# Dealing out anew the side work of the attention heads in a fused attention and mixture-of-experts block

## The reference

```python
q, k, v = x @ Wq.T, x @ Wk.T, x @ Wv.T          # x is layer-normed; q 512 wide, k and v 128 wide
scores = einsum('bsqhd,bthd->bqhst', qh, kh) * scale   # 8 key heads of 16, 4 query groups each
a_dot  = einsum('bqhst,bthd->bsqhd', softmax(scores), vh)
sigma_q = elu(q.reshape(b, s, 4, 128))
a_mem  = sigma_q @ memory / (sigma_q @ memory_norm)
x = x + a_dot * (1 - w) + a_mem * w             # w = sigmoid(memory_weight)
# then: layernorm, router (sigmoid, top 4 of 16 experts), experts of 192, shared expert, sum
```

## Time and profile before

| | us |
|---|---|
| median of 3 executions | 1956.91 (1956.83 to 1957.64) |
| the profiled execution | 1947.51 |
| its span, first to last instruction | 1945.6 |
| PE busy | 1872.0 (96%) |
| DVE busy | 1031.1 (53%) |
| ACT busy | 978.7 (50%) |
| POOL busy | 921.2 (47%) |

### The profile page before, as it was taken

How to read it: one execution, slowest core, us unless ns; L and a number is a source line. 1 busy time by engine, 2 the same in 40 slices (tenths; PEclk the granted TensorE clock), 3 DMA queues, 4 the chain that set the end, 5 groups by cost and what they waited for, 6 DMA issues and landing times. The chain is left out here.

```text
span 1945.6 us, 34872 instructions
## 1 busy us (share of the span) xinstructions
PE 1872.0 (96%) x9240; PEld 965.8 (50%) x9241; DVE 1031.1 (53%) x1995; ACT 978.7 (50%) x1901; POOL 921.2 (47%) x1127
## 2 busy tenths in 40 slices
PE   6899999999999999999999899999999999999996
PEld 5444445444544454445333455555555555555553
DVE  5667777878787878787888252222221222222213
ACT  3366776677667766776766532223332233322330
POOL 3533566666666766675633650333333333333342
PEclk9799999999999999999999999999999999999998
DMA  6422334434443444333532897877777777777779
GB/s 193 108 70 64 83 94 132 128 107 116 132 134 103 116 131 135 104 103 120 150 120 82 290 342 237 183 142 141 141 144 142 142 141 141 143 143 141 142 164 262
DMA packets 159128, 277.71 MB, mean 143 GB/s; under 512 B 28704, under 2 KB 64800, under 8 KB 156256
## 3 DMA queue, kind: packets, MB, share of 16 engines
q1 hardware_dynamic: 108688, 147.61, 26.7%
q0 software_dynamic: 40880, 106.96, 26.6%
q10 hardware_dynamic: 9440, 21.68, 3.2%
HBM read 145.65 MB, written 135.74 MB: 145 GB/s over the span
## 5 line engine op out<-in xcount | busy, mean ns | idle before, releaser
L993 DVE TENSOR_REDUCE mx<-ps_max 128x2 f32<-128x1024 f32 x512 | 618.1, 1219 | 174.7 <-PE ps_max L1203 160.6
L732 ACT ACTIVATE prob<-ps_exp 128x512 f32<-128x512 f32 x992 | 566.9, 598 | 149.2 <-PE ps_exp L1217 131.6
L1948 PE MATMUL ps_gu<-wts_sb,xT 128*128 x1152 | 402.7, 493 | 1.2 <-issue 1.0
L1217 PE MATMUL ps_exp<-qs,ks 98*128 98x512 bf16 x992 | 380.0, 383 | 18.9 <-ACT prob L732 16.7
L1647 POOL DMA_INDIRECT out<-yt,idx x72 | 111.7, 1551 | 467.6 <-ACT yt L1716 453.2
L1203 PE MATMUL ps_max<-ks,qs 96*128 96x512 bf16 x1024 | 310.2, 385 | 7.5 <-DVE mx L993 4.0
L1828 DVE COPY hT<-ps_h 128x384 f32<-128x384 f32 x88 | 49.1, 557 | 463.2 <-PE ps_h L1957 463.2
L1948 PEld LDWEIGHTS ps_gu<-wts_sb,xT 128*128 128x128 f32 x1152 | 207.3, 190 | 170.9 <-issue 56.4
L1245 PE MATMUL ps_pv<-prob,vs 128*32 128x512 f32 x2048 | 251.8, 605 | 0.2 <-ACT prob L740 0.2
L1706 ACT ACTIVATE gs<-ps_gu 128x192 f32<-128x192 f32 x176 | 58.2, 330 | 376.4 <-PE ps_gu L1948 376.4
L1217 PEld LDWEIGHTS ps_exp<-qs,ks 98*128 98x128 bf16 x992 | 96.8, 98 | 195.7 <-ACT prob L732 88.5
(11 more groups left out here) (197 smaller groups left out, 2177.2 us busy)
## 6 DMA issues: line engine op xcount, KB each, us to landing
xt<-rows_by_expert SPq DMA_DIRECT2D x144, 264.5 KB, 2.7
dnr_sb<-in_dnr SPq DMA_DIRECT2D x144, 128.0 KB, 2.6
qk_parts<-parts POOLq DMA_DIRECT2D x112, 120.0 KB, 3.6
qs<-qk_parts SPq DMA_DIRECT2D x64, 192.0 KB, 3.1
wts_sb<-in_wts ACTq DMA_DIRECT2D x12, 1024.0 KB, 8.3
x_sb<-in_x SPq DMA_DIRECT2D x16, 512.0 KB, 4.5
qs<-qk_parts SPq DMA_DIRECT2D x64, 128.0 KB, 3.1
x_plus_memory<-am SPq DMA_DIRECT2D x16, 512.0 KB, 5.2
```

The source lines that it names most:

```text
L732: act.activation(prob[:, s, q], ps_exp[:, q % 2], ACT.Exp, scale=SCALE).then_inc(s_exp, 1)
L993: dve.tensor_reduce(mx[:, k % 2, 4 * s + 2 * p:4 * s + 2 * p + 2], ps_max[:, p], AX_X, ALU.max).then_inc(s_maxd, 1)
L1217: pe.matmul(ps_exp[:, q % 2], ks[0:ROWS + MROWS, kk, s * P:(s + 1) * P], qs[0:ROWS + MROWS, kk, q], start=True, stop=True).then_inc(s_sc, 1)
L1948: mm = pe.matmul(ps_gu[:, i, 0:2 * I], xT[:, i, d], w, start=(d == 0), stop=(d == DC - 1))
```

## The change

No arithmetic changes but for padding: the maxima's transposes become 128 wide, with zeros, where they were 32 wide. What changes is where work stands.

- **Transposed maxima.** `mb` is 128 wide (a memset more at the start), `max_T` writes into `ps_pv` and not `ps_misc`, and waits for ACT's copy of `ps_pv` (`s_oT`); the next `pv` at p = 4 waits for ACT's copy of the maxima (`s_mT`).
- **`o_T` and `o_out`** go from p = 3 to p = 2 in ordinary heads, `o_T` right behind `max_T`.
- **Rows' transposes.** `a_T` goes from places -12 and -11 (20 and 21) to -12 and -8 (20 and 24), `c_T` stays at 4 and 8; all stand ahead of the place's `pv` on PE (`ahead_of_pv`), where they stood behind it, and ACT copies them right behind the place's exponentials (`behind_exps`).
- **Values.** One piece of eight products at place -7 becomes three: two products each at -11 and -10 (first half of the rows) and four at -7.
- **Keys.** Two products each at -1 and 1 become one each at -3, -2, -1 and 1.
- **Logits.** Eight products at 9 become four at 9 and four at 11 (`logits_at`), with an exponential of 16 columns each on ACT.
- **Memory read.** Three rounds of 3, 3 and 2 products at 23, 28 and 29 become four rounds of 2 at 17, 19, 23 and 27; DVE has four copies for three. The first two rounds need only the first half of sigma.
- **ACT.** The second step of the elu (`below`) goes from 8.5 and 16.5 to right behind its first (7.5 and 15.5), ahead of `oT_out`.
- **DVE.** `weights` (four small linked instructions) goes from place 19 to 21.

```diff
-MEM = 3
+MEM = 4
-    mb = sb("mb", [P, 2, 2, 16], BF16)
+    mb = sb("mb", [P, 2, P], BF16)
-    USUAL = LAST | {"rank": 16}
+    USUAL = LAST | {"rank": 16, "weights": 21}
...
-    MEM_ROUNDS = [[(0, 0), (0, 1), (0, 2)], [(0, 3), (1, 0), (1, 1)], [(1, 2), (1, 3)]]
+    MEM_AT = (17, 19, 23, 27)
+    MEM_ROUNDS = [[(0, 2), (0, 3)], [(1, 2), (1, 3)], [(0, 0), (0, 1)], [(1, 0), (1, 1)]]
...
-                pe.wait_ge(s_sig, 2 * a + 2)
+                pe.wait_ge(s_sig, 2 * a + (1 if n < 2 else 2))
...
+                    pe.wait_ge(s_mT, min(g, NG))
...
             def max_T(g, k):
-                free_misc()
+                if g >= 3:
+                    pe.wait_ge(s_oT, g - 2)
                 pe.wait_ge(s_mb, g)
-                pe.transpose(misc_b[0:32, 0:P], mb[:, (k + 1) % 2].rearrange("p a n -> p (a n)"), identb[:]).then_inc(s_mTp, 1)
-                set_free(s_mT, g)
+                pe.transpose(pv_b[:, 0:P], mb[:, (k + 1) % 2], identb[:]).then_inc(s_mTp, 1)
...
+                        if p in (0, 4):
+                            at(ahead_of_pv(8 * k + p))
...
-                        if p == 2 and runs(g, 1, NG + 1):
-                            max_T(g, k)
-                        if p == 3 and runs(g, 3, NG + 3):
-                            o_T(g)
+                        if p == (3 if alone(g) else 2):
+                            if runs(g, 1, NG + 1):
+                                max_T(g, k)
+                            if runs(g, 3, NG + 3):
+                                o_T(g)
```

More of the change, by code:

```diff
@@ L144, in attention @@
     ps_pv = lent_ps("ps_pv", [P, SEQ])
-    misc_b = ps_misc[:, :].bitcast(BF16)
+    pv_b = ps_pv[:, :].bitcast(BF16)
     BANK_OF_T = [[ps_misc[:, :], ps_max[:, 0, 0]], [ps_max[:, 0, 1], ps_max[:, 1, 0]]]
@@ L711, in xn2T_out, with exp_logits @@
                                ACT.Copy).then_inc(s_xn2T, 1)
[L713 to L716, removed]
+            def exp_logits(t):
+                act.wait_ge(s_lg, 2 * c + (t + 1 if c < NU - 3 else 2))
+                act.activation(rt[:, 0, t], ps_misc[:, t * E:(t + 1) * E], ACT.Exp, scale=-1.0).then_inc(s_el, 1)
             at = places_of(c)
-            return {at["T"][0]: [lambda: xn2T_out(0)], at["T"][1]: [lambda: xn2T_out(1)], at["logits"]: [exp_logits]}
+            first, second = (behind_exps(p) if c < NU - 3 else p for p in at["T"])
+            return logits_at(c, exp_logits) | {first: [lambda: xn2T_out(0)], second: [lambda: xn2T_out(1)]}
         def body(b):
@@ L769, in body @@
                         at(8 * k + p)
-                        if p == 2 and runs(g, 1, NG + 1):
+                        if p == (3 if alone(g) else 2) and runs(g, 1, NG + 1):
                             mT_out(g, k)
@@ L1017, in body @@
                             maxima(g, k, s, half_)
-                        if p == 3 and runs(g, 3, NG + 3):
+                        if p == (3 if alone(g) else 2) and runs(g, 3, NG + 3):
                             o_out(g, k)
@@ L1069, in front @@
                     split(a, chunk)
-            for p in (23, 28, 29):
+            for p in MEM_AT:
                 for task in of_a(0)[p]:
@@ L1127, in a_q, with a_k @@
                     set_free(s_qf, 3 * a + (3, 2)[j])
[L1129 to L1131 removed]
+            def a_k(i):
+                if i == 0:
                     free_misc()
[L1133 to L1134 removed]
                     pe.wait_ge(s_xnT, 2 * a + 2)
[L1136 to L1138 removed]
+                mm = pe.matmul(ps_misc[:, 0:UT], w_sb[:, i, D:D + P], xnT[:, i], start=(i == 0), stop=(i == DC - 1))
+                if i == DC - 1:
                     mm.then_inc(s_proj, 1)
@@ L1188, in of_c @@
             at = places_of(c)
-            return {at["T"][0]: [lambda: c_T(0)], at["T"][1]: [lambda: c_T(1)], at["logits"]: [c_logits],
+            first, second = (ahead_of_pv(p) if c < NU - 3 else p for p in at["T"])
+            return logits_at(c, c_logits) | {first: [lambda: c_T(0)], second: [lambda: c_T(1)],
                     between_halves(at["rank"]) if c < NU - 3 else at["rank"]: [c_rank]}
```

122 lines of the change are left out of this document (63 added, 59 removed).

## The result

| | before | changed |
|---|---|---|
| median, us | 1957.28 (4 executions) | 2015.47 (2014.44 to 2020.14, 4 executions) |
| ratio | | 1.0298, 95% interval 1.0278 to 1.0318 |
| profiled execution / its span | 1947.51 / 1945.6 | 2014.67 / 2012.8 |
| PE, DVE, ACT, POOL busy | 1872.0, 1031.1, 978.7, 921.2 | 1881.3, 1043.0, 1005.1, 923.2 |

The forecast was 2008 in a range of 1970 to 2020. PE is busy for only 9 us more, and the span is 67 us longer: the time went into waits.

The account below looks back on a forecast made before the run. PE bounds the heads, busy 63.73 of 64.75 us; an ordinary block grows 4.5 to 69.2. Blocks 3 to 12 add 45, block 13 4, 14 and 15 3.5, 0 to 2 -1: +51 on 1956.9 gives 2008, range 1970 to 2020.

Parts of the forecast that it names:

- places 0 to 4: Block start: rows of c ahead of `pv` wait 2.7 us for POOL's norm; place 5 comes 2.3 later.
- 5 to 11, with the wait at 11: Copies, halved logits, maxima and a wait of 0.6 at place 11 make this stretch 0.4 us later.
- 17 to 20: Places 1.8, 1.7, 1.9 and 3.7 through waits for the bank and DVE; block 1.6 us later at place 21.
- 21 to 24: Weights and maxima delay DVE's memory copy; PE waits 1.5 at place 24; block 3.1 behind at 25, from 1.6.
- 25 to 31: Fewer values products, no memory at 28 and 29, and single keys, less a wait at 27: 1.3 us back.
- not stretched: Rival: chain at the block's start not stretched, wait at place 4 only 1.4, block 3.2 longer, 1995 us; chance 0.18.
- faster: Rival: PE finds the bank free at place 3, about 2.5 a block gained in 11 blocks, 1926 us; chance 0.08.
- DVE's queue is shorter: Rival: waits at 20 and 24 (1.9) fall to 0.5, block about 1.7 longer, 1977 us; chance 0.14.
- Four heads give back 0.6: Transposed maxima without 32-column products cost PE 0.11 for 0.26 a head, 0.6 us less a block.
- the order undone by the last units: Worse rival: the last units' other tables cost at most 10 us more, 2018 us; chance 0.08.
- The start stays: The kernel's start, like the experts, was taken to keep its time.
- About 35 us is the most that any dealing could give back: Upper limit from PE's waits of 2.7 us a block, in 10 full blocks and half a dozen with less.

Follow-up runs that it names:

- e1: Changed kernel with the first of unit c's two row transposes (place 4) back behind `pv`, ACT's copy too: 1971.8 us, ratio 1.014.
- e2: Changed kernel with POOL's addition of x at place 26, ahead of three scatters, not at 31: 1976.4 us, ratio 1.017.
- e7: Changed kernel with the edits of e1, e2 and e3 together: 1949.6 us, ratio to before 0.9975.
- e3: Changed kernel with DVE's weights at place 20 rather than 21: 1989.7 us, ratio 1.023.
- e5: Changed kernel with memory read in three rounds at 23, 28 and 29, not four at 17, 19, 23 and 27: 1993.5 us, ratio 1.024.
- e4: Kernel before plus only the 128-wide maxima transposes written into the bank of `pv`: 1944.5 us, ratio 1.0005.
- b7: b5 without the addition of 1e-20 to the sum of the chosen weights: 1917.8 us, ratio to before 0.9855.
- b1: e4 plus the elu's second step right behind its first: 1952.3 us, ratio to before 0.998.
- b4: Changed kernel re-dealt by who empties the bank: `o_T` at 3, most rows behind `pv`, memory at 17, 23, 28, weights at 20: 1955.5 us, ratio 0.9998.
- b6: b4 with DVE's weights at place 19 rather than 20: 1920.3 us, ratio to before 0.987.
- b5: b6 with DVE's copy of the ranks ahead of the maxima of place 16: 1960.7 us, ratio to before 1.008.

## Why the prediction was right

The range held the time and the sign was that of the 0.90. Point by point, a full block, us (measured: means of blocks 4 to 12, block 10 with a held product included):

| step | predicted | measured |
|---|---|---|
| places 0 to 4 | +2.3 | +3.2 (+2.4 where the clock stayed) |
| 5 to 11, with the wait at 11 | +0.4 | +0.4 (2.42 at place 11) |
| 17 to 20 | +1.6 | +1.4 |
| 21 to 24 | +1.5 | +2.1 |
| 25 to 31 | -1.3 | -1.2 |
| block | 69.2 | 69.2 to 69.8 in blocks 5, 8, 12; 70.8 to 71.1 in five; 72.5 in block 10 |

- **Places 0 to 4: the mechanism, the size and the stretched chain are shown.** The wait was put at 2.7, and the place takes 5.90 for 3.31 where the clock stayed. The addition ends 2.91 after the block's start where the prediction had 2.95, and the split ends 1.26 later than before, priced at 1.2. e1 takes the position away; e2 takes the whole hold of the split away (1.78 us), and the wait falls by 1.25, place 3 by 0.28. The rival "not stretched" is out.
- **The waits for DVE's copies behind `o_T`** at 11 and 19 came as counted: place 19 takes 1.94 for 1.9. Place 11 takes 2.42, which is 0.88 of products, about 1.0 of logits (what place 9 lost) and a wait of 0.5 for the 0.6 of the sum. The condition of the rival "faster", 1.4 us from a maximum's start to the end of `o_out`, is refuted: it is 1.97 (559.01 to 560.98), where the prediction read 2.0, and PE stands 0.37 for `o_all` at place 19. In e7 both places keep these lengths.
- **Place 24** takes 4.88 in most blocks, 2.06 more than before; the sum's 0.88 of products, wait of 1.5, 0.44 of rows and 1.95 of `pv` make 4.77. e3 shows that the weights' place is what costs. "DVE's queue is shorter" is out.
- **Places 17 to 20**: 1.50, 1.77, 1.94, 3.56 for 1.8, 1.7, 1.9, 3.7, and e5 gives the 1.8 us back.
- **The maxima: the step failed.** "Four heads give back 0.6" took PE's cost for the place's length. The product costs less than I took (0.06 for 0.11), and yet e4 gives back only 0.05 in a block: at place 18 PE waits for ACT 0.39 where it waited 0.29, at 26 it stands 0.13 for 0.03, at 2 0.04 for nothing, and 10 comes down to the 1.07 under which no place goes. The 0.6 is spread over four groups of places, so none of them misses by more than 0.2 for it.
- **What the sum lacked: the clock.** Blocks 4 to 12 all have the pause of 2.19 us at place 4; behind five of the nine PE ran at half clock for 3.41 us, and place 4 took 7.0 to 7.6 for 5.9. That is 1.4 x 5 = 7 of the 9.4 by which the 54.4 of blocks 3 to 12 exceed the 45. Block 10, with the held product and half clock behind it, adds 3.1; block 3, only 2.2 longer than before since its place 4 takes 4.35, takes off 2.3; the rest is in tenths.
- **The ends.** Blocks 14 and what drains cost 15.4 for 3.5: "the order undone by the last units", with 10 us more at most, was the right worry (11.9 more), at half clock from 1131 to 1138 and 1158 to 1165; that its mechanism is the order of these units was not tried alone. "The start stays" was wrong by 7.7; 6.6 of it are in block 0, which takes 57.8 for 64.4. In e5, with memory late, block 0 takes 59.1, so memory's early rounds are not what makes most of it. They tell only in its second half (31.1 for 35.3; 35.7 in e5). The rest of the cause is open.
- **The sum against the median.** +67 by the two profiled executions, +58 by the medians: before's profiled execution stood 9.8 under its median of 1957.28, after's 0.8 under. The prediction's +51 was 16 too small against the trace and 7 against the median.
- **How near the number came is in part luck.** By the trace the blocks 3 to 12 were 9.4 short, block 13 1.9 and the end 11.9; the start and blocks 1 and 2 took back 7.5, and the medians lie 9 nearer than the traces. What is earned is the mechanism of a full block where the clock stayed, 69.2 to 69.8 for 69.2. The 2015.5 itself lies nearer to the 2018 of the worse rival than to the 2008.
- **The range's chance** of "0.82 or so" is 0.86 by the chances given: 0.5, 0.18, 0.14 and half of 0.08.
- **"About 35 us is the most that any dealing could give back"** stands: b7 gives 28.8.

The Trainium skill, "SBUF — State Buffer", "SBUF: two separate sides", says that a VectorE operation with two SBUF inputs and a GpSimd operation that reads SBUF exclude each other, the loser blocking. The traces agree: only operations with two such inputs were held (`mb` 1.95, `rt` up to 4.37, `wk` up to 4.31, 0.16 to 0.3 otherwise), the reductions and reciprocals between them never.

## What to carry to other kernels

When side work shares one bank, deal it by who empties the bank and by what stands ahead of that copy on its engine, not by how evenly it fills the matrix engine; a copy behind a reduction of 1.2 us needs 2.9 us to its next user, and a consumer moved ahead of long products turns its producer's lateness into a stop of everything. A tiny two-input VectorE instruction beside GpSimd arithmetic is a risk of microseconds: look for the longest, not the mean, of each small group, and move it, or rewrite it with one input. Before shortening something inside a step, ask what paces the step. Compare whole runs at both ends too, not typical blocks alone: start and end moved by 7.7 and 15.4 us here.

## What the runs showed of the hardware

- **A pause doesn't always lower TensorE's clock.** The same pause (2.17 to 2.19 us) came in each of blocks 4 to 12; the granted clock fell to the 1.2 GHz level for 3.41 us behind five of them. Neither is a pause needed: b1 has four stretches at half clock (264, 459, 653, 848) behind blocks without any; PE's own rows were gapless for 9 us before the first. What sets them off there is open. The table of stages of b1:

```profile
255.00:264.00 9.00, 9.00 (x59) 5.10 (x58) 5.13 (x8) 6.66 (x13) 6.49 (x10) 1.00 0.38 110
264.00:267.50 3.50, 3.50 (x12) 1.74 (x11) 2.99 (x4) 2.16 (x6) 2.94 (x4) 0.55 0.01 2
```

- **A held instruction can lose several times in a row.** It passed between two of POOL's operations (at 501.00 in e5), or only behind the fifth (4.37 us in b4). Once POOL's next arithmetic was 0.74 us off in the records, it passed in b6 and was held in b5; POOL was issuing DMAs meanwhile. The records of POOL's sequencer tell the two apart. Behind `sig` in its program stands a wait for a semaphore, which the sequencer reaches only once it has sent `sig` off. Of the two-input steps of the weights that start up to 2.5 us ahead of `sig` in all fourteen traces, 19 were held, and in each of them the sequencer had passed that wait 0.10 to 0.40 us before; 147 ran freely, and in each it passed the wait 0.02 us after their start or later. The recorded start of `sig` does not tell: it was 0.23 to 0.98 ahead in the held ones, and as little as 0.26 in the free ones. So by the records it is the sending off that counts. No run moved it alone. Why one was released behind `sig` and another only behind the fifth operation stays open.
- **A wide transpose is nearly free beside other full-width products**: 0.06 us for 128 columns of bfloat16, where the 32-wide one cost 0.26.
